# Cross-attention of a decoder layer: value transposes and per-query inverses taken off TensorE, inverses by log, exp and a Newton step

## The reference

```
x = x + attn(layernorm(x))                # 16 heads of 128, rotary, causal window 256
x = x + cross(layernorm(x), context)      # 8 heads over the channel axis
x = x + experts(layernorm(x))             # 16 experts, top-k tokens, one shared weight
```

```
qh = layernorm(x).reshape(16, 8, 32, 512);  kh = vh = context.reshape(16, 8, 32, 512)
qk = einsum('bhdq,bhdl->bhql', qh, kh) / sqrt(32)
ret = einsum('bhql,bhdl->bhdq', softmax(qk, axis=-1), vh);  out = gamma * ret
```

## Time and profile before

| | |
|---|---|
| three runs | 2761.4, 2759.67, 2757.46 us; median 2759.67 |
| profiled execution | 2760.93 us, span 2759.2 |
| granted clock of PE | 0.978 of full speed in the mean |
| busy of the span | PE 2626.3 us (95%), DVE 1755.7 (64%), ACT 985.4 (36%), GpSimd (POOL) 861.7 (31%) |
| DMA | 272.28 MB, 99 GB/s in the mean, all through the queue that SP issues to |

### The profile page before, as it was taken

How to read it: one execution, slowest core, us unless ns; L and a number is a source line. 1 busy time by engine, 2 the same in 40 slices (tenths; PEclk the granted TensorE clock), 3 DMA queues, 4 the chain that set the end, 5 groups by cost and what they waited for, 6 DMA issues and landing times. The chain is left out here.

```text
span 2759.2 us, 38367 instructions
## 1 busy us (share of the span) xinstructions
PE 2626.3 (95%) x13448; PEld 1973.6 (72%) x13448; DVE 1755.7 (64%) x3663; ACT 985.4 (36%) x2469; POOL 861.7 (31%) x698
## 2 busy tenths in 40 slices
PE   6999999999999999999999999999599999999794
PEld 5888888888888888888887888888344444444683
DVE  5777776665655665655665665666467776665557
ACT  2332223222222323222232222222267777776220
POOL 3211112221211322111132221111268887777000
PEclk9999999999999999999999999999699999999797
DMA  3123223222211323211122311110567676662003
GB/s 115 62 92 108 107 77 126 73 82 102 77 61 62 100 69 117 82 62 62 62 100 93 114 62 62 62 62 31 176 180 186 186 185 181 183 181 62 20 1 122
DMA packets 162476, 272.28 MB, mean 99 GB/s; under 512 B 11504, under 2 KB 78064, under 8 KB 162288
## 3 DMA queue, kind: packets, MB, share of 16 engines
q1 hardware_dynamic: 162288, 269.82, 31.6%
HBM read 176.98 MB, written 92.27 MB: 98 GB/s over the span
## 5 line engine op out<-in xcount | busy, mean ns | idle before, releaser
L346 PE MATMUL pj<-xnt,whi 128*128 128x512 f32 x2048 | 705.8, 406 | 5.1 <-DVE xnt L580 5.1
L439 ACT ACTIVATE pr<-sc,nmx 128x128 f32<-128x128 f32 (+1 forms) x512 | 211.1, 417 | 929.0 <-DVE nmx L525 929.0
L291 POOL TENSOR_TENSOR qt<-rot,swp 128x512 f32<-128x512 f32 x128 | 166.0, 1297 | 1107.2 <-DVE swp L505 1107.2
L346 PEld LDWEIGHTS pj<-xnt,whi 128*128 128x128 f32 x2048 | 387.0, 189 | 97.9 <-DVE xnt L580 5.8
L979 DVE TENSOR_REDUCE xnmx<-xsc 128x1 f32<-128x512 f32 x512 | 336.4, 684 | 163.2 <-PE xsc L799 160.2
L346 PE MATMUL pj<-xnt,wlo 128*128 128x512 f32 x1024 | 399.7, 390 | 0.0
L769 POOL TENSOR_TENSOR xprt<-xprt 128x512 f32<-128x512 f32 x256 | 320.2, 1280 | 119.8 <-PE xob L819 91.0
L343 PE MATMUL pj<-whi,xnt 128*128 128x512 f32 x1024 | 352.9, 406 | 4.0 <-issue 4.0
L921 ACT ACTIVATE xprt<-xst 128x512 f32<-128x512 f32 x512 | 290.6, 596 | 112.3 <-PE xst L808 108.8
L503 DVE TENSOR_TENSOR rot<-pj,trig 128x512 f32<-128x512 f32 x256 | 176.6, 690 | 212.5 <-PE pj L346 212.5
L799 PE MATMUL xsc<-kst,qst 96*128 96x512 f32 x512 | 235.4, 464 | 34.2 <-DMA kst<-sk_scratch 31.7
(11 more groups left out here) (190 smaller groups left out, 4341.8 us busy)
## 6 DMA issues: line engine op xcount, KB each, us to landing
xnt<-xt_scratch SPq DMA_DIRECT2D x48, 1024.0 KB, 7.5
x_scratch<-xio SPq DMA_DIRECT2D x64, 512.0 KB, 3.6
xio<-x_scratch SPq DMA_DIRECT2D x48, 512.0 KB, 4.1
qst<-sq_scratch SPq DMA_DIRECT2D x96, 256.0 KB, 5.0
kst<-sk_scratch SPq DMA_DIRECT2D x96, 256.0 KB, 5.7
raw<-in_w_all_dram SPq DMA_DIRECT2D x64, 256.0 KB, 4.7
xt_scratch<-xnt SPq DMA_DIRECT2D x16, 1024.0 KB, 8.8
sq_scratch<-qp SPq DMA_DIRECT2D x32, 512.0 KB, 8.1
```

Of the source, the lines that this page charges most:

```text
L291: nc.gpsimd.tensor_tensor(qk["QK".index(kind)][h][:, :, :].rearrange("p b n -> p (b n)"), rot[r % 2][:, :], swp[r % 2][:, :], ALU.add).the ...
L346: last = nc.tensor.matmul(bank[:, :], wpart[:, w, i * HD:(i + 1) * HD], moving, start=(k == 0), stop=(k == 3 * CB - 1))
L439: nc.scalar.activation(pr[:, a % 4, lo:hi], SC[a % 2][:, lo:hi], ACT.Exp, bias=nmx[:, a % 4, t:t + 1], accum_out=rsum[:, a % 4, t:t + 1]). ...
```

## The change

- The context comes a second time as input, turned by the host's reshaping into `ctx_t` (tile, 128, 4, 128), and `load_values` reads a tile of it straight into `vt`, now with three buffers. `values` and `v_evac` go.
- The sums are no longer turned. ACT takes their logarithm (`log_of_sums`) and exp(-log) (`inverse_of_sums`), and DVE refines with one Newton step in place in the bank of the sums (`newton`, `newton_end`). `sums_by_query`, `inverses`, `sums_evac`, `repeat` and `one_over_sums` go; there are two banks for sums in place of `SU` and `VB`. gamma is multiplied in `output_evac`.
- `weigh` moves from the end of the step to its middle, and `sums` from the middle of steps 0 and 2 to their end.
- `qp` and `kp` have two buffers each, the ring of `prt` has 6 in place of 5.
- The standard deviations are inverted on DVE alone (a first guess by shifting bits, four Newton steps); the square root goes. One ACT table set with log and exp is named at the stage's start.
- The stacks stay as they are: three parts in three neighbouring blocks of 32 partitions.

```diff
-        RING = 5
+        RING = 6
...
-        qp = sb("qp", [P, 2, D], F32R)
-        kp = sb("kp", [P, 2, D], F32R)
+        qp = [sb(f"qp{i}", [P, 2, D], F32R) for i in range(2)]
+        kp = [sb(f"kp{i}", [P, 2, D], F32R) for i in range(2)]
...
-        vt = sb("vt", [P, 2, CB, P], F32)
+        vt = sb("vt", [P, 3, CB, P], F32)
...
-        SU = pb("xsu")
-        VB = pb("xvb")
+        SU = [pb(f"xsu{i}") for i in range(2)]
...
             def load_context(m):
                 if m >= 4:
-                    sp.wait_ge(s_vt, m - 3)
                     sp.wait_ge(s_klo, m - 3)
                 sp.dma_start(cin[:, m % 4, :], cv[m]).then_inc(s_ci[m % 4], 16)
 
+            def load_values(m):
+                if m >= 3:
+                    sp.wait_ge(s_pv, CB * (m - 2))
+                sp.dma_start(vt[:, m % 3, :, :], ctx_t[m]).then_inc(s_vt[m % 3], 16)
...
                 if tile(n + 3):
                     write_queries(n + 3)
                     write_keys(n + 3)
+                if tile(n + 2):
+                    load_values(n + 2)
...
             def sums(n, k):
                 pe.wait_ge(s_add, XPT * (2 * n + k + 1))
-                if k == 0:
-                    pe.wait_ge(s_se, n)
+                if k == 0 and n >= 2:
+                    pe.wait_ge(s_on, n - 1)
                 for h in range(XPT):
                     rows = slice(XD * h, XD * (h + 1))
-                    last = nc.tensor.matmul(SU[rows, :], ones[:, :], prt[(CB * n + 2 * k) % RING][:, h, :],
+                    last = nc.tensor.matmul(SU[n % 2][rows, :], ones[:, :], prt[(CB * n + 2 * k) % RING][:, h, :],
                                             start=(k == 0), stop=(k == 1))
                 last.then_inc(s_su, 1)
...
                         transposed_scores(s, i)
-                    if i == 1:
-                        middle(s // CB, s % CB)
-                if 0 <= s - 1 < STEPS:
-                    weigh(s - 1)
+                    if i == 1 and s % CB == 2 and tile(s // CB + 1):
+                        max_transposes(s // CB + 1)
+                    if i == 1 and 0 <= s - 1 < STEPS:
+                        weigh(s - 1)
+                if s % CB in (0, 2) and tile(s // CB - 1):
+                    sums(s // CB - 1, s % CB // 2)
 
...
-            rstd_of_all(nc, act, None, rstd, tmp, s_var, s_sqrt, s_step, scale=XSCALE)
+            nc.scalar.preload_act_table_set("natural_log_exp_and_others")
...
             def q_round(m):
                 act.wait_ge(s_qn, m + 1)
-                act.wait_ge(s_qw, 16 * m)
-                nc.scalar.activation(qp[:, 0, :], xn[:, :], ACT.Copy).then_inc(s_qhi, 1)
+                if m >= 2:
+                    act.wait_ge(s_qw, 16 * (m - 1))
+                nc.scalar.activation(qp[m % 2][:, 0, :], xn[:, :], ACT.Copy).then_inc(s_qhi, 1)
...
             def output_evac(n):
                 act.wait_ge(s_pv, CB * n + CB)
                 if n >= 2:
                     act.wait_ge(s_on, n - 1)
-                nc.scalar.activation(osb[n % 2][:, :], OB[:, :], ACT.Copy).then_inc(s_oe, 1)
-
-            def sums_evac(n):
+                nc.scalar.activation(osb[n % 2][:, :], OB[:, :], ACT.Copy, scale=gam[:, 0:1]).then_inc(s_oe, 1)
+
+            def log_of_sums(n):
                 act.wait_ge(s_su, 2 * n + 2)
-                act.wait_ge(s_sq, n)
-                nc.scalar.activation(ssb[:, :], SU[:, :], ACT.Copy).then_inc(s_se, 1)
+                act.wait_ge(s_new, 2 * n)
+                nc.scalar.activation(rin[:, :], SU[n % 2][:, :], ACT.Ln).then_inc(s_log, 1)
+
+            def inverse_of_sums(n):
+                act.wait_ge(s_log, n + 1)
+                nc.scalar.activation(rin[:, :], rin[:, :], ACT.Exp, scale=-1.0).then_inc(s_inv, 1)
...
-            WORK = {(0, 0): ((k_round, 3),), (0, 1): ((repeat, -2),), (0, 2): ((v_evac, 0),), (1, 0): ((output_evac, -1),),
-                    (1, 1): ((normed, 4),), (1, 3): ((q_round, 4),), (2, 2): ((max_round, 1),), (2, 3): ((sums_evac, -1),)}
+            WORK = {(0, 0): ((k_round, 3),), (0, 2): ((output_evac, -1),), (1, 1): ((normed, 4),), (1, 3): ((q_round, 4),),
+                    (2, 2): ((max_round, 1),), (3, 0): ((log_of_sums, -1),), (3, 2): ((inverse_of_sums, -1),)}
...
-            nc.vector.tensor_scalar(tmp[:, 0, :], mv2[:, :, 1], EPS, None, ALU.add).then_inc(s_var, 1)
-            dve.wait_ge(s_var, 1)
-            rstd_of_all(nc, None, dve, rstd[:, :], tmp, s_var, s_sqrt, s_step, scale=XSCALE)
+            steps = [0]
+
+            def step(ins):
+                steps[0] += 1
+                ins.then_inc(s_step, 1)
+                dve.wait_ge(s_step, steps[0])
+
+            step(nc.vector.tensor_scalar(var[:, :], mv2[:, :, 1], EPS, None, ALU.add))
+            step(nc.vector.tensor_scalar(seed[:, :], var[:, :].bitcast(I32), 1, None, ALU.logical_shift_right))
+            step(nc.vector.tensor_scalar(rstd[:, :].bitcast(I32), seed[:, :], -1.0, float(0x5f3759df), ALU.mult, ALU.add))
+            for _ in range(4):
+                step(nc.vector.scalar_tensor_tensor(half[:, :], rstd[:, :], -0.5, rstd[:, :], ALU.mult, ALU.mult))
+                step(nc.vector.tensor_tensor(half[:, :], half[:, :], var[:, :], ALU.mult))
+                step(nc.vector.scalar_tensor_tensor(rstd[:, :], half[:, :], 1.5, rstd[:, :], ALU.add, ALU.mult))
+            step(nc.vector.tensor_scalar(rstd[:, :], rstd[:, :], XSCALE, None, ALU.mult))
             nc.vector.scalar_tensor_tensor(shift[:, :], mv2[:, :, 0], -1.0, rstd[:, :], ALU.mult, ALU.mult).then_inc(s_shift, 1)
...
-            def one_over_sums(n):
-                dve.wait_ge(s_sq, n + 1)
-                dve.wait_ge(s_rr, n)
-                nc.vector.reciprocal(rq[:, :], VB[:, 0:CB * XPT]).then_inc(s_ri, 1)
+            def newton(n):
+                dve.wait_ge(s_inv, n + 1)
+                nc.vector.scalar_tensor_tensor(SU[n % 2][:, :], SU[n % 2][:, :], -1.0, rin[:, :],
+                                               ALU.mult, ALU.mult).then_inc(s_new, 1)
+
+            def newton_end(n):
+                dve.wait_ge(s_new, 2 * n + 1)
+                nc.vector.scalar_tensor_tensor(SU[n % 2][:, :], SU[n % 2][:, :], 2.0, rin[:, :],
+                                               ALU.add, ALU.mult).then_inc(s_new, 1)
 
             def output(n):
-                dve.wait_ge(s_rt, n + 1)
+                dve.wait_ge(s_new, 2 * n + 2)
+                dve.wait_ge(s_oe, n + 1)
                 dve.wait_ge(s_x2, n)
-                nc.vector.tensor_tensor(onm[:, :], osb[n % 2][:, :], VB[:, :], ALU.mult).then_inc(s_on, 1)
+                nc.vector.tensor_tensor(onm[:, :], osb[n % 2][:, :], SU[n % 2][:, :], ALU.mult).then_inc(s_on, 1)
...
-            WORK = {(0, 1): ((statistics, -3),), (0, 2): ((mean_and_variance, -3),), (2, 0): ((output, -2),),
-                    (2, 2): ((max_rest, 1),), (3, 3): ((one_over_sums, -1),)}
+            WORK = {(0, 0): ((statistics, -3),), (0, 1): ((newton, -2),), (0, 2): ((mean_and_variance, -3),),
+                    (0, 3): ((newton_end, -2),), (1, 1): ((output, -2),), (2, 2): ((max_rest, 1),)}
...
+    ctx_t = _np.asarray(inputs["ctx_2048"]).reshape(TILES, P, CB, P).transpose(0, 3, 2, 1)
```

More of the change, by code:

```diff
@@ L33 @@
 CH_Q, CH_K, CH_V, CH_O = 0, CB, 2 * CB, 3 * CB
[L36 to L55, removed]
 def self_attention(nc, x, w_all, rope, xt, x1, mv2, cst):
@@ L637, in cross_attention @@
         gam = sb("gam", [P, 1], F32)
-        tmp = sb("rs_tmp2", [P, 2, TILES], F32)
+        var = sb("var2", [P, TILES], F32)
+        seed = sb("seed2", [P, TILES], I32)
+        half = sb("half2", [P, TILES], F32)
         rstd = sb("rstd2", [P, TILES], F32)
@@ L677, in cross_attention @@
         s_mt, s_mhi, s_mlo = sem("x_mt"), sem("x_mhi"), sem("x_mlo")
-        s_vt, s_vte = sem("x_vt"), sem("x_vte")
+        s_vt = [sem(f"x_vt{i}") for i in range(3)]
         s_ts, s_exp = sem("x_ts"), sem("x_exp")
         s_pv, s_add, s_su = sem("x_pv"), sem("x_add"), sem("x_su")
-        s_oe, s_se = sem("x_oe"), sem("x_se")
-        s_sq, s_ri, s_rr, s_rt = sem("x_sq"), sem("x_ri"), sem("x_rr"), sem("x_rt")
+        s_oe = sem("x_oe")
+        s_log, s_inv, s_new = sem("x_log"), sem("x_inv"), sem("x_new")
         s_on, s_x2, s_bn = sem("x_on"), sem("x_x2"), sem("x_bn")
@@ L813, in weigh @@
                 pe.wait_ge(s_exp, 4 * s + 4)
-                pe.wait_ge(s_vte, n + 1)
+                pe.wait_ge(s_vt[n % 3], 16 * (n // 3 + 1))
                 if c == 0:
@@ L818, in weigh @@
                     rows = slice(XD * h, XD * (h + 1))
-                    last = nc.tensor.matmul(OB[rows, :], vt[:, n % 2, c, rows], prt[s % RING][:, h, :],
+                    last = nc.tensor.matmul(OB[rows, :], vt[:, n % 3, c, rows], prt[s % RING][:, h, :],
                                             start=(c == 0), stop=(c == CB - 1))
@@ L844, in max_transposes @@
                 nc.tensor.transpose(MX[0:XPT * CB, 0:P], nmx[:, n % 2, :], ident[:, :]).then_inc(s_mt, 1)
```

(29 more changed lines are left out.)

34 lines of the change are left out of this document (13 added, 21 removed).

## The result

The changed kernel took 2778.81 us (median of 6 runs, 2772.21 to 2783.7) against 2759.14 us for the kernel before on the same chip (6 runs). The ratio is 1.007, 95% interval 1.0053 to 1.0087: slower by 0.7%, outside my range and opposite to my sum of 2757.

A forecast was written before the change was run, and what follows sets the result against it. It took a closed loop of stack reads and PE through one buffer, 17.25 us a tile, as the bound. Steady loops +4.4, start +2.4, first tiles -2.5, end -6.8 gave -2.5: median 2757 us, range 2746 to 2771.

The forecast's parts named there:

- The closed loop: Cross-attention: stack read, score, transposed score and freeing of one buffer set nearly every tile, 17.25 us each.
- The path, 7.33: From first score of c = 2 to last transposed score of c = 3: 7.33 us, against 7.01 without stalls before.
- +0.17 a tile: Steady tiles: +0.32 on the path less 0.15 of q_round's stalls; +4.4 us over 26 loops.
- A wait of about 1.7 a tile takes the place of the removed work: PE in steps c = 0 and 1: 8.2 us of work against 9.9 until the stacks land, so 1.7 of waiting.
- rival 4: Steady tiles: the new wait lowers PE's clock, the path loses 1.7 a tile, +44 us, 2801; chance 0.05.
- Start, +2.4: Stage start, first DVE step to end of shift: 6.1 us where it was 3.7, all later work waiting.
- First tiles, -2.5: Tiles 0 to 2, filling the pipeline: q_round no longer stands before the exponentials, -2.5 us (bounds 0 and -4).
- End, -6.8: Tiles 30, 31 and stage tail: -1 and -1.7, earlier weigh -2, shorter output -2.1; bounds -3 and -9.
- Stalls of q_round, the second Exp and Ln, DVE's Newton steps, the extra load: Steady tiles: q_round's waits go, 0.15 a tile gained; the added ACT, DVE and transfer work costs nothing.
- Rivals 3 and 5: Step c = 3: Ln delays a transposed score, 2769, chance 0.14; Ln and Exp each load their table, 2814, 0.02.
- Rival 2: Steady tiles: PE bounds, each step costs its fullest engine's load, 16.4 a tile, -22 us, 2731; chance 0.06.

The follow-up runs named there:

- fill6: The changed kernel plus six extra matmuls of 384 columns, results unused, at the end of step c = 1 of every tile: 2767.7 us, ratio 1.0039.
- weigh_end: The changed kernel with weigh back at the end of the step and output_evac one sub-step later: 2759.46 us, ratio 1.0005.
- before_mid: The kernel before with only weigh moved to the middle of the step, all transposes kept: 2844.33 us, ratio 1.032.
- Experiment 8: The changed kernel with four stack buffers and POOL's memsets moved behind the first two remainders of the queries: 2719.99 us, ratio 0.9869.
- fill3: The changed kernel plus three extra matmuls of 384 columns, results unused, at the end of step c = 1: 2769.16 us, ratio 1.0042.

## Why the prediction was wrong, step by step

- **The closed loop**: right. Periods without a fall add up as read; in every tile from 3 on of the kernel after and of fill6 the first score starts 0.04 to 0.05 after the last stack has landed; fill6 puts work into c = 1 and the period doesn't grow; a fourth buffer takes it from 17.4 to 16.0.
- **The path, 7.33**: right as a sum, 7.28 to 7.35 in 17 of the 25 tiles from 7 on. Its two terms, 0.88 for sums_by_query and 1.2 for the moved block, are not shown one by one, and that they came out is in part luck: from weigh_end to fill6 the block adds 0.51 (6.80 to 7.31), from before to weigh_end the path loses 0.42 (7.22 to 6.80), and in the order of before_mid the block adds 1.9. What a block costs depends on what stands around it. **+0.17 a tile**: right where the clock holds. The 24 tiles from 7 on took 16.4 more, less eight falls of 1.55 that is 4.0, or +0.17 each; in fill6, without falls, it is +0.13 (417.05 against 414.05).
- **"A wait of about 1.7 a tile takes the place of the removed work"**: right, 1.6. This is the step that failed, because my sum put its price at nothing. Half clock came behind that wait in ten tiles and cost 1.55 each on the path, 15.5 us, where my total had zero; with the wait filled (fill6) the kernel takes 2767.7, inside my range, though still above the kernel before. It is rival 4. I priced it at 1.7 a tile, which was close, but in all 26 tiles, and gave it 0.05 with one reason: in the earlier trace rows the clock fell after a gap of over 2 us. One row where the clock falls shows a sufficient case; it does not show that a shorter wait is safe, and I had set no row of a wait of 1 to 2 us at full clock against it. Both ends of the range, none and every tile, should have been kept, with a third as open as the rest. The Trainium skill (TensorE: Matmul & The Clock Gate, "HAM oscillation") describes the mechanism, a DMA wait in every tile behind which PE starts at the lower clock; here it is seen in a third of the tiles, not in each, and with waits of 1.4 to 2.6 us, shorter than those of its example. What decides which of two like waits ends in a fall stays open.
- **Start, +2.4**: too low, +3.5 to the first read. Seed and first guess took 1.82 each where I had 0.6 (bound 1.4). The row to doubt was my own term: 1.43 for an operation on 32 columns beside 0.19 for the next is no duration of the operation, but POOL's memset beside it. Experiment 8 shows it. The Trainium skill (SBUF — State Buffer, "Who interferes with whom") says that tensor_scalar has two-port modes that use the port pair shared with GpSimd, and that whoever issues first then holds the pair for the whole instruction. The common ends fit that, and so does the kernel before, where a tensor_tensor beside a memset took its usual 0.19; runs here show only that the memsets cause it, not the port.
- **First tiles, -2.5**: wrong, +1.2 to the read of tile 3, without a fall. It lies in the round from the read of tile 2 to that of tile 3 (16.67 to 18.14), and there in the path, 5.76 to 7.20; weigh_end, with the weighing at the end of the step, has 5.75. So the moved block costs already in the first tiles, where I had put no loop, and q_round's stall gave back nothing like 2.5.
- **End, -6.8**: -4.6. From the last transposed score to the next stage 16.8 became 12.06, -4.7 where I had -4.1. The -2.7 for tiles 30 and 31 did not come (+0.2).
- **Stalls of q_round, the second Exp and Ln, DVE's Newton steps, the extra load**: right. From 2104 to 2540 us no wait for any of them is listed, and the stage has only one table load (1.28 at 1962.67). Rivals 3 and 5 are out.
- **Rival 2** (16.4 a tile by the engines' loads) was wrong for three buffers and nearly right for four: 16.03.

In one sum: my parts gave -2.5. Ten falls +15.5, start +1.1, first tiles +3.7, the other loops -0.9 (+3.5 for +4.4), end +2.2 and -0.1 behind the stage make it +19.0. The last 3.4 of the 22.4 are self-attention, a difference of executions and not of the change.

## What to carry to other kernels

Work that you take from an engine inside a closed loop comes back as a wait, and a wait on TensorE can have a price of its own: when the new wait is over a microsecond per round (1.33 was the shortest here with a fall behind it), or when many small matmuls follow even a short one, keep half clock on the path behind it as an open case, and look at the granted clock by stretches as the first thing after. Open the loop first (one more buffer) and shorten the work then; the same edit cost 0.7% in one order and gained 0.6% in the other. And where an operation of 32 columns takes over a microsecond, look at what runs beside it before using the number.

## What the runs showed of the hardware

- In the kernel after and fill3 the granted clock fell to half after single waits of 1.33 to 2.55 us in a loop of 17.4 us (PE busy 374 of 414 us), though not after each. In fill6, with waits of at most 1.25 us, it did not fall once before the tail. Each fall in the kernel after cost 1.55 us on the path; six matmuls with unused results, in the wait, avoided all.
- In before_mid it fell 16 times with no wait over 0.71 us: each time after a wait of 0.45 to 0.47 and eight matmuls of 128x4, though not after each such pair. That waits are short does not keep the clock up.
- VectorE's tensor_scalar on 128x32 took 0.18 us alone and 1.43 to 1.82 beside a GpSimd memset of 1.80, and ended 0.04 after it each time. The first operation of the earlier trace rows, 1.43, ends at 1961.16, 0.04 after the first of the three memsets in the kernel before, which starts at 1959.32 (POOL's timeline there). The three tensor_tensor operations beside the memsets in that kernel took 0.19:

```profile
1959.32 5.51 POOL L776 MEMSET kst<- 2x2048 f32 x3 [30.74 <-POOLq L63]
```
